# Reordered instruction streams of the gated-delta (first recurrent) layer in a four-engine pipeline

## The reference, cut to what matters

```python
q = silu(causal_dwconv(x @ Wq, qcw, qcb))       # 4 taps; k and v alike
k = k.reshape(B, T, H, DK) * DK ** (-0.5)
alpha, beta = sigmoid(x @ Wa + ba), sigmoid(x @ Wb + bb)
def step(S, inps):
    qt, kt, vt, at, bt = inps
    err = einsum('bhvk,bhk->bhv', S, kt) - vt
    S = at * S - bt * (err[..., None] * kt[:, :, None, :])
    return S, einsum('bhvk,bhk->bhv', S, qt)
o = (o - mean(o)) * rsqrt(var(o) + 1e-05) * ln_w + ln_b
return (o * sigmoid(x @ Wg)) @ Wo
```

## Time and profile before

| what | value |
|---|---|
| runs | 3175.97, 3179.49, 3179.65 us; median 3179.49 |
| the profiled execution | 3177.65 us, span 3175.9 us, mean granted PE clock 0.991 |
| busy PE / PEld / DVE / ACT / POOL | 97% / 80% / 64% / 52% / 39% |
| the layer that the change touches | PE from 402.4 us (first projection) to about 1870 us |

### The profile page before, as it was taken

One profiled execution on the slowest core, in us unless ns is written; L12 is line 12 of the kernel. 1 busy time (PEld: TensorE's weight loads), 2 busy tenths in 40 slices (PEclk: granted clock), 3 DMA queues, 4 the chain that ended last, 5 costly groups with the idle time before them and its releaser, 6 DMA issues. The chain is left out here.

```text
span 3175.9 us, 61451 instructions
## 1 busy us (share of the span) xinstructions
PE 3094.5 (97%) x23984; PEld 2550.1 (80%) x23984; DVE 2044.6 (64%) x3598; ACT 1648.3 (52%) x3880; POOL 1245.6 (39%) x2223
## 2 busy tenths in 40 slices
PE   8999989999999999999999999999999999999998
PEld 6888868888888888888788778778888888888887
DVE  5212267778777787777777743655666666666666
ACT  4221357777777777777777743343433333222222
POOL 2322335555455555555455434422333322222212
PEclk9999999999999999999999989999999999999999
DMA  2100121111111111111111145410010111000004
GB/s 89 33 21 26 60 66 37 49 45 55 51 48 45 55 50 44 51 51 45 51 48 45 54 137 162 130 44 31 27 30 27 31 43 33 24 21 27 24 17 159
DMA packets 130243, 165.70 MB, mean 52 GB/s; under 512 B 9936, under 2 KB 72144, under 8 KB 129920
## 3 DMA queue, kind: packets, MB, share of 16 engines
q1 hardware_dynamic: 120592, 144.49, 14.8%
q10 hardware_dynamic: 9296, 17.04, 1.5%
q0 software_dynamic: 64, 0.23, 0.0%
HBM read 127.91 MB, written 33.82 MB: 51 GB/s over the span
## 5 line engine op out<-in xcount | busy, mean ns | idle before, releaser
L1466 DVE SCALAR_TENSOR_TENSOR b_zt<-b_rx,b_cw,b_zt 128x512 f32<-128x512 f32 x576 | 472.2, 820 | 24.0 <-POOL b_rx L1665 4.0
L70 PE MATMUL bank<-b_XH,b_wh 128*128 128x512 f32 x1024 | 468.6, 458 | 13.1 <-ACT b_zt L1222 11.7
L72 PE MATMUL bank<-b_XH,b_wl 128*128 128x512 f32 x1024 | 405.5, 396 | 0.0
L71 PE MATMUL bank<-b_XL,b_wh 128*128 128x512 f32 x1024 | 403.0, 394 | 0.0
L70 PE MATMUL bank<-b_XH,b_qh 128*128 128x512 f32 x1024 | 399.3, 390 | 1.4 <-DVE b_g L2580 1.4
L71 PE MATMUL bank<-b_XL,b_qh 128*128 128x512 f32 x1024 | 398.9, 390 | 0.0
L72 PE MATMUL bank<-b_XH,b_ql 128*128 128x512 f32 x1024 | 398.7, 389 | 0.0
L2679 POOL TENSOR_TENSOR b_QHL<-b_qhd,b_QHH 128x512 fp32r<-128x512 f32 x128 | 181.8, 1424 | 476.4 <-ACT b_QHH L2458 474.0
L1710 POOL TENSOR_TENSOR b_PR<-b_A,b_T 128x15 f32<-128x15 f32 (+7 forms) x480 | 179.6, 374 | 188.3 <-issue 153.3
L2458 ACT CAST b_QHH<-b_qhd 128x512 fp32r<-128x512 f32 x128 | 79.5, 623 | 308.0 <-PE bank L72 186.4
L72 PEld LDWEIGHTS bank<-b_XH,b_wl 128*128 128x128 f32 x1024 | 193.2, 189 | 44.8
(11 more groups left out here) (249 smaller groups left out, 7567.3 us busy)
## 6 DMA issues: line engine op xcount, KB each, us to landing
b_abc<-tmp_a SPq DMA_DIRECT2D x64, 256.0 KB, 3.8
b_gbc<-tmp_g SPq DMA_DIRECT2D x64, 256.0 KB, 3.8
tmp_og<-b_gg SPq DMA_DIRECT2D x64, 256.0 KB, 2.1
b_mo<-tmp_og SPq DMA_DIRECT2D x64, 256.0 KB, 3.1
b_wr<-in_Wk SPq DMA_DIRECT2D x16, 256.0 KB, 4.3
b_wr<-in_Wq SPq DMA_DIRECT2D x16, 256.0 KB, 4.6
b_wr<-in_Wv SPq DMA_DIRECT2D x16, 256.0 KB, 2.6
b_wr<-in_Wg SPq DMA_DIRECT2D x16, 256.0 KB, 2.7
```

The lines of the kernel that those rows point to most:

```text
L70: e.do.matmul(out, wh, xh, start=first and k == 0, stop=False)
L71: e.do.matmul(out, wh, xl, start=False, stop=False)
L72: m = e.do.matmul(out, wl, xh, start=False, stop=last and k == n - 1)
L1466: e.do.scalar_tensor_tensor(out=z[:, :], in0=rx[:, j:j + 512], scalar=cw[:, u // 2, KIND[name[0]], j:j + 1], in1=z[:, :], op0=ALU.mult, op ...
```

## The change

Every engine's list is permuted; no instruction is added, removed or resized. The loops of PE, ACT, POOL and SP also start at another point of the round, and so does DVE's, which then needs one round less; that by itself leaves the order of the instructions as it was. What differs once that turning is taken out:
- **Projections**: same cyclic order (k0, g1, v0, q0, k1, q1, v1, g0). Banks 0 to 3 are dealt out anew.
- **PE**: `scores(2)` and `scores(3)` come ahead of and behind `inverse8_second`, before `turn(0)`; `chain2(0)` moves behind piece 3 of g0; `turn_kv(3)` moves from behind piece 3 of k0 to ahead of `chain3(0)`; `turn_kv(1)` moves up to `chain2(1)`; `turn_kv(2)` moves up to `chain1(3)`; `chain2(3)` one projection piece up; `chain3(3)` directly behind `chain4(3)`, ahead of `inverse3`.
- **DVE**: the decays spread differently; `gated(1)` ahead of `chain3(1)`; `chain3(3)` ahead of `taps(q0)`.
- **POOL**: `decayed_q(1)` of a unit moves from behind `decayed_q(0)` to a place between the first and second `root` of the following round; `root(2)` now stands ahead of `cut_next("q")` (before: behind it); `cut_next("g")` moves from ahead of `decayed_q(1)` to behind the next `rows(14)`; `cut_next("v")` and `decayed_q(0)` stay last ahead of `rows(0)`; `ones` moves behind the roots.
- **ACT**: `finish("k1")`, `finish("q1")` ahead of `out7(1)`; `cut_next` calls moved; `turned(1)` and `turned_kv(3)` ahead of `chain4(0)`; `sums(0)`, `sums(1)` together ahead of `turned_kv(0)`.
- **SP**: `products(1)` of a unit moves one round later, `decays(0)` of the next unit stands ahead of `products(0)`.

```diff
@@ -685,12 +685,12 @@
 
 
 
-PROJECTIONS = (("q1", 1), ("v1", 1), ("g0", 2), ("k0", 0), ("g1", 2), ("v0", 0), ("q0", 0), ("k1", 0))
+PROJECTIONS = (("g0", 2), ("k0", 0), ("g1", 2), ("v0", 0), ("q0", 0), ("k1", 0), ("q1", 0), ("v1", 0))
 
 TURNS = (
-    ("kv2", 2, 2), ("s3", 2, 0), ("s4a", 2, 2), ("s5", 2, 2), ("sc0", 1, 0), ("s6", 2, 2),
-    ("s7a", 2, 1), ("s78", 2, 2), ("sc1", 1, 3), ("turn0", 3, 0), ("sc2", 1, 1), ("sc3", 1, 0),
-    ("turn1", 3, 2), ("kv3", 2, 0), ("kv0", 1, 3), ("kv1", 1, 2),
+    ("sc0", 1, 3), ("s6", 2, 0), ("s7a", 2, 1), ("s78", 2, 2), ("sc1", 1, 0), ("sc2", 1, 1),
+    ("sc3", 1, 3), ("turn0", 3, 0), ("kv3", 2, 1), ("turn1", 3, 0), ("kv0", 1, 3), ("kv1", 1, 2),
+    ("kv2", 1, 3), ("s3", 1, 2), ("s4a", 1, 0), ("s5", 1, 1),
 )
 ROUNDS = NU + 3
 P_ORDER = [(i - lag, n) for i in range(ROUNDS) for n, lag in PROJECTIONS if 0 <= i - lag < NU]
@@ -891,17 +891,17 @@
     e.wait_ge("dn", 48)
     for i in range(NU + 4):
         store(i - 4, 0)
-        decays(i - 1, 0)
+        decays(i - 1, 1)
         store(i - 4, 1)
         ahead(i - 3, 1)
         ahead(i - 2, 0)
+        load_next("k", i - 1)
+        products(i - 2, 1)
+        load_next("q", i - 1)
         load_next("v", i - 1)
-        decays(i - 1, 1)
+        decays(i, 0)
         products(i - 1, 0)
         load_next("g", i - 1)
-        products(i - 1, 1)
-        load_next("k", i)
-        load_next("q", i)
 
 
 def attn0_pe(e, k, t, mt):
@@ -1117,26 +1117,6 @@
             mix0_out(e, k, mt, 0, c, js)
 
     for i in range(NU + 3):
-        project(i - 1, "q0", 2, 3)
-        chain2(i - 3, 3)
-        ahead(i - 3, 3)
-        project(i - 1, "q0", 3, 4)
-        project(i - 1, "k1", 1, 2)
-        turn_kv(i - 2, 2)
-        project(i - 1, "k1", 2, 3)
-        chain4(i - 3, 3)
-        project(i - 1, "q1", 0, 1)
-        inverse3(i - 2)
-        chain3(i - 3, 3)
-        ahead(i - 3, 4)
-        project(i - 1, "q1", 1, 2)
-        inverse4(i - 2, 0, 4)
-        project(i - 1, "k1", 3, 4)
-        project(i - 1, "q1", 2, 3)
-        inverse4(i - 2, 4, 8)
-        project(i - 1, "q1", 3, 4)
-        project(i - 1, "v1", 0, 1)
-        inverse5(i - 2)
         scores(i - 1, 0)
         inverse6(i - 2)
         project(i - 1, "v1", 1, 2)
@@ -1148,30 +1128,30 @@
         inverse78(i - 2)
         scores(i - 1, 1)
         project(i - 2, "g0", 1, 2)
+        scores(i - 1, 2)
         inverse8_second(i - 2)
+        scores(i - 1, 3)
         turn(i - 3, 0)
-        scores(i - 1, 2)
+        project(i - 2, "g0", 2, 3)
         chain2(i - 2, 0)
-        scores(i - 1, 3)
-        project(i - 2, "g0", 2, 3)
         project(i, "k0", 0, 1)
+        turn_kv(i - 2, 3)
         chain3(i - 2, 0)
         chain4(i - 2, 0)
         project(i, "k0", 1, 2)
         turn(i - 3, 1)
         project(i - 2, "g0", 3, 4)
+        project(i, "k0", 2, 3)
         chain1(i - 2, 1)
-        project(i, "k0", 2, 3)
-        turn_kv(i - 2, 3)
         project(i, "k0", 3, 4)
+        turn_kv(i - 1, 0)
         chain2(i - 2, 1)
-        turn_kv(i - 1, 0)
+        turn_kv(i - 1, 1)
         project(i - 2, "g1", 0, 1)
         chain4(i - 2, 1)
         chain3(i - 2, 1)
         project(i, "v0", 0, 1)
         project(i - 2, "g1", 1, 2)
-        turn_kv(i - 1, 1)
         chain1(i - 2, 2)
         project(i, "v0", 1, 2)
         project(i - 2, "g1", 2, 3)
@@ -1182,12 +1162,32 @@
         chain4(i - 2, 2)
         chain3(i - 2, 2)
         ahead(i - 2, 1)
+        project(i, "q0", 0, 1)
         project(i, "v0", 3, 4)
-        project(i, "q0", 0, 1)
         chain1(i - 2, 3)
         ahead(i - 2, 2)
+        turn_kv(i - 1, 2)
         project(i, "q0", 1, 2)
+        chain2(i - 2, 3)
+        ahead(i - 2, 3)
+        project(i, "q0", 2, 3)
         project(i, "k1", 0, 1)
+        project(i, "q0", 3, 4)
+        project(i, "k1", 1, 2)
+        chain4(i - 2, 3)
+        chain3(i - 2, 3)
+        ahead(i - 2, 4)
+        project(i, "k1", 2, 3)
+        project(i, "q1", 0, 1)
+        inverse3(i - 1)
+        project(i, "q1", 1, 2)
+        inverse4(i - 1, 0, 4)
+        project(i, "k1", 3, 4)
+        project(i, "q1", 2, 3)
+        inverse4(i - 1, 4, 8)
+        project(i, "q1", 3, 4)
+        project(i, "v1", 0, 1)
+        inverse5(i - 1)
 
 
 def attn0_act(e, k, t, mt):
@@ -1392,59 +1392,59 @@
     e.wait_ge("dn", 48)
     for i in range(NU + 3):
         sums(i - 3, 0)
-        chain4(i - 3, 1)
-        turned_kv(i - 2, 1)
-        finish(i - 2, "v1")
+        sums(i - 3, 1)
+        turned_kv(i - 2, 0)
         chain2(i - 3, 2)
         ahead(i - 3, 1)
+        ahead(i - 3, 2)
+        turned_kv(i - 2, 1)
         gate(i - 3, 1)
-        sums(i - 3, 1)
-        ahead(i - 3, 2)
         chain4(i - 3, 2)
-        taken(i - 1, "v0")
         sums(i - 3, 2)
         ahead(i - 3, 3)
+        taken(i - 1, "v0")
+        finish(i - 1, "k0")
         cut_next("k", i - 1)
-        finish(i - 1, "k0")
+        chain2(i - 3, 3)
+        ahead(i - 3, 4)
         spread(i - 2, 0)
         spread(i - 2, 1)
-        chain2(i - 3, 3)
-        ahead(i - 3, 4)
         taken(i - 1, "q0")
+        turned_kv(i - 2, 2)
+        chain4(i - 3, 3)
+        out3(i - 2)
         finish(i - 1, "v0")
-        turned_kv(i - 2, 2)
-        out3(i - 2)
-        chain4(i - 3, 3)
         sums(i - 3, 3)
         ahead(i - 3, 5)
         taken(i - 1, "k1")
         finish(i - 1, "q0")
+        cut_next("q", i - 1)
         taken(i - 1, "q1")
         out5(i - 2)
-        cut_next("q", i - 1)
         lower4(i - 2)
         placed6(i - 2)
         placed4(i - 2)
         out7(i - 2, 0)
-        cut_next("v", i - 1)
-        out7(i - 2, 1)
         finish(i - 1, "k1")
         finish(i - 1, "q1")
+        out7(i - 2, 1)
+        cut_next("v", i - 1)
+        taken(i - 1, "v1")
         placed8(i - 2)
         ahead(i - 2, 0)
         turned(i - 3, 0)
-        taken(i - 1, "v1")
         chain2(i - 2, 0)
-        cut_next("g", i - 1)
         diagonal(i - 1, 0)
         diagonal(i - 1, 2)
+        turned_kv(i - 2, 3)
+        turned(i - 3, 1)
         chain4(i - 2, 0)
-        turned(i - 3, 1)
         gate(i - 2, 0)
         chain2(i - 2, 1)
+        cut_next("g", i - 1)
         taken(i, "k0")
-        turned_kv(i - 2, 3)
-        turned_kv(i - 1, 0)
+        chain4(i - 2, 1)
+        finish(i - 1, "v1")
 
 
 def attn0_dve(e, k, t, mt):
@@ -1599,49 +1599,49 @@
     for d in range(3):
         i = e.do.memset(t[f"D{d}"][:, 0:1], 0.0)
     i.then_inc(S["ini"], 1)
-    for i in range(NU + 3):
-        chain1(i - 2, 0)
-        scaled(i - 3, 0)
-        masked(i - 1, 0)
-        masked(i - 1, 1)
-        decay(i - 1, 3)
-        masked(i - 1, 2)
-        masked(i - 1, 3)
-        decay(i - 1, 4)
-        decay(i - 1, 5)
-        decay(i - 1, 6)
-        masked(i - 1, 4)
-        masked(i - 1, 5)
-        decay(i - 1, 7)
-        masked(i - 1, 6)
-        masked(i - 1, 7)
-        scaled(i - 3, 1)
-        gated(i - 3, 0)
-        chain3(i - 2, 0)
-        sixteens(i - 1)
-        chain1(i - 2, 1)
-        taps(i - 1, "v1")
+    for i in range(NU + 2):
         chain3(i - 2, 1)
-        gated(i - 3, 1)
+        decay(i, 0)
         chain1(i - 2, 2)
         ahead(i - 2, 0, 1)
+        decay(i, 1)
         taps(i, "k0")
         chain3(i - 2, 2)
         ahead(i - 2, 1, 2)
         chain1(i - 2, 3)
         ahead(i - 2, 2, 4)
+        decay(i, 2)
         taps(i, "v0")
-        decay(i, 0)
         blocks(i - 1)
-        decay(i, 1)
-        decay(i, 2)
+        chain3(i - 2, 3)
+        ahead(i - 2, 4, 6)
         taps(i, "q0")
         first_guess(i - 2)
-        chain3(i - 2, 3)
-        ahead(i - 2, 4, 6)
         added4(i - 1)
         taps(i, "k1")
         taps(i, "q1")
+        chain1(i - 1, 0)
+        scaled(i - 2, 0)
+        masked(i, 0)
+        masked(i, 1)
+        decay(i, 3)
+        masked(i, 2)
+        decay(i, 4)
+        decay(i, 5)
+        masked(i, 3)
+        masked(i, 4)
+        decay(i, 6)
+        decay(i, 7)
+        masked(i, 5)
+        masked(i, 6)
+        masked(i, 7)
+        scaled(i - 2, 1)
+        gated(i - 2, 0)
+        chain3(i - 1, 0)
+        sixteens(i)
+        chain1(i - 1, 1)
+        taps(i, "v1")
+        gated(i - 2, 1)
 
 
 def attn0_pool(e, k, t, mt):
@@ -1743,39 +1743,39 @@
 
     e.wait_ge("dn", 48)
     for i in range(NU + 3):
+        rows(i - 2, 0)
+        rows(i - 2, 2)
+        tail(i - 2, "v1")
         rows(i - 2, 4)
         rows(i - 2, 6)
         halo(i - 1, "v0")
         rows(i - 2, 8)
-        tail(i - 1, "k0")
         rows(i - 2, 10)
         rows(i - 2, 12)
+        rows(i - 2, 14)
+        tail(i - 1, "k0")
+        cut_next("g", i - 2)
         halo(i - 1, "q0")
-        rows(i - 2, 14)
+        off_diagonal(i - 2)
         tail(i - 1, "v0")
-        off_diagonal(i - 2)
+        cut_next("k", i - 1)
         tail(i - 1, "q0")
         halo(i - 1, "k1")
-        cut_next("k", i - 1)
-        ones(i - 1)
-        halo(i - 1, "q1")
```

(18 more changed lines are left out.)

## The result

The changed kernel takes 3153.41 us, the median of 6 runs (3149.00 to 3156.89), beside 3178.33 for the kernel before on the same chip (6 runs, 3174.30 to 3179.65): a ratio of 0.9924, 95% interval 0.9915 to 0.9934, or 24.9 us less. Forecast were 3165 and a range of 3157 to 3176.

The account below looks back on a forecast made before the run. PE, busy 97%, was taken as the bound, losing time in weight rounds waiting at turn(1) for DVE's scaled(1). Terms -14.7 + 1 + 0 = -13.7 us on 3177.65 gave 3164.0, stated as 3165 for run spread; range 3157 to 3176.

Parts of the forecast that it names:

- the third root: POOL's late root(2) delays scaled(0) by 0.67 us, but masked waits for PE anyway: costs the kernel nothing.
- Term 1: POOL's collision with DVE's scaled(1) in 14 weight rounds: the 1.05 us wait at turn(1) goes, -14.7 us.
- term 5: Fill and tail: 0 us, bounds -2 and +2 each; PE's 4.4 us of waits without releaser may change by -3 to +3.
- Term 2: PE's own stream, new neighbours of steps: about +0.03 us a round, +1 us in all, bounds -16 and +7.
- Term 3: Serial chain, gaps from chain1 to chain2 of chunks 1 and 3 shrink to 1.6 us: 0 us, bound +19.
- Its rival: Slower through the short chain gap: sixteens still runs on DVE when chain1(1) delivers, R(1) late; 3196 us, chance 0.10.
- Term 4: Other moved calls on POOL, SP and ACT: each has slack enough, so 0 us.
- 2: The collision moves instead of going, scaled(1) late in all rounds: 3182 us, or 3174 in half the rounds; chance 0.15.
- 3: The short gap in the chain makes DVE's R(1) late: 31 us for 1 us a round, 3196 us; chance 0.10.
- Rival 4: Smaller or larger gain: PE's own stream comes out at its low half, or stalls without releaser vanish; 3158 us, chance 0.08.

Follow-up runs that it names:

- root_ahead: The kernel before with only root(2) moved ahead of cut_next("q") on POOL: 3178.83 us, ratio 1.0004 to the kernel before.
- g_away: The kernel before with only POOL's cut_next("g") moved behind the next rows(14): 3164.29 us, ratio 0.9957 to the kernel before.
- product_thrice: The changed kernel with POOL making decayed_q(0) three times, same values: 3198.34 us, ratio 1.0063 to the kernel before.
- after_again: The changed kernel, unchanged, executed once more for a second profile: 3148.36 us.
- pe_act_back: The changed kernel with PE's and ACT's lists (and PE's tables) of before; DVE, POOL and SP stay changed: 3178.68 us, ratio 1.0006 to the kernel before.
- root_behind: The changed kernel with root(2) put back behind cut_next("q") on POOL: 3150.37 us, ratio 0.9917 to the kernel before.
- pe_back: The changed kernel with PE's list and two tables of before, other engines as changed: 3220.23 us, ratio 1.0134 to the kernel before.
- scores_together: The changed kernel with scores(3) right behind scores(2), both ahead of inverse8_second, on PE alone: 3150.99 us, ratio 0.9915 to the kernel before.
- after_shift: The changed kernel with 128 already-met semaphore waits put ahead of PE's list: 3154.37 us, ratio 0.9927 to the kernel before.

## Why the prediction was right and wrong

- **What bounds the kernel, and the third root**: right. PE in weight rounds was the only steady loss; the third root costs nothing (root_ahead 1.0004).
- **Term 1**: the mechanism was right, `scaled(1)` ends beside a product in all rounds, 2.08 us long, with slack (g_away, product_thrice), and the wait is gone. The size was short, and this is the first of the two steps that failed (the other is in term 5): it took 1.05 us a weight round from the wait at `turn(1)`, and the rounds gave 1.34, so 18.8 us and not 14.7. The late `scaled(1)` made PE slow a second time, at `chain2(1)`, in a row of the weight loads' waits that the prediction had not read; that is 0.11 of the missing 0.29 us. The prediction also named the wrong neighbour: the first operation beside the slow `scaled(1)` was the low part of g, and moving that alone gave 1.19 us a round (g_away). It had the better number before it: the two windows of the earlier trace rows differ by 1.32 us, at an equal number of matmuls, and only 1.05 of that was explained. Had the sum taken the whole of it as the price of a weight round, the forecast would have been about 3161.
- **Term 2**: right. Forecast +0.03 us a round, measured +0.04 in the rounds without weights, and -0.02 in after_again, so not to be told from nothing; `scores(2)` 0.955 and `scores(3)` 0.968 against 0.96 each; `turn(0)` and `chain2(0)` fell by 0.14 and 0.08.
- **Term 3**: right at 0, but closer than it looked: R of chunk 1 has 0.3 us to spare in the rounds without weights and 0.02 to 0.14 in the weight rounds, where the walk had left 0.4. Its rival is real, too: pe_act_back shows it at 1.2 us a weight round as soon as one cast stands in the wrong place.
- **Term 4**: the sum is right and the reasoning was not. It counted each move of ACT and SP at nothing by the slack of the kernel before, as if they were independent. The four mixed kernels show that they are the other halves of the moves on PE and POOL: PE's new list among the old ones costs 55 us, PE's and ACT's new lists among the old ones 63; PE's old list among the new ones costs 67; and with PE's and ACT's old lists among the new ones all of the gain is lost.
- **Term 5**: too small, the second step that failed. The fill gave 1.4 us and is real (109.1 to 110.0 in four further executions of changed lists, 110.2 to 112.5 in five with the old ones): a product left the side of the first taps, and the granted clock came back sooner. The tail gave 0.4. The stalls without releaser gave 4.4, over the bound of 3: the row L983 alone, 4.4 us, was read for all of them, while start to start there were 10.0, and 4.3 of these in one round, which has no like in the changed kernel. Of the 10.2 us by which the profiled execution beat the sum (23.9 against 13.7), term 1 is 4.1, the stalls are 4.4, fill and tail 1.8, and all else -0.1.
- **Rivals**: 2 and 3 did not come. Rival 4 named the direction and, with 3158, was nearest. Of its two reasons, term 2 at its low end did not happen; the stalls shrank by 4.4 us, but didn't vanish, and the rest came from term 1 and the fill. The range was too narrow below since its low end took term 1 as capped by one wait. It doesn't hold what it says either: the low bound of term 2 alone, -16, would have led to 3148 and the high bound of term 3, +19, to 3184, while the range ends at 3157 and 3176. With term 1 at its measured 18.8 the sum gives 3161, inside the range; it takes the stalls and the fill to leave it.

The stalls' 4.4 us are not an effect that the change aims at: they go by which step stands at a place of PE's stream, and perhaps by what the other engines do then (pe_back, pe_act_back). Another order with the same merits could lose them again; this is luck as far as the forecast goes.

No version tried beats the changed kernel by more than its interval: root_behind and scores_together lie 3.0 and 2.4 us below, after_shift 1.0 above.

## What to carry to other kernels

When two kinds of round do the same work, the difference of their lengths is the price to explain, to the last tenth; a wait read from one row is only a part of it, and the weight loads' waits are to be read beside the matmuls'. To find what holds an operation up, begin the other engine's timeline ahead of the operation's start, not in its middle. Behind a long stall look at the granted clock as well, and then at whether a later wait takes up what it costs. In a kernel with one hand-written list for each engine, a move that "costs nothing" is often what another move needs: test the smallest part alone (here one POOL call gave half the gain), and don't expect one engine's new list to run with the others' old ones. A large elementwise product on POOL is placed by what DVE runs beside it, not by POOL's own idle time.

## What the runs showed of the hardware that was not expected

Which DVE work a POOL operation holds up depends on its kind. Timelines of DVE and POOL, changed kernel, ahead of the round at 1253.43:

```profile
1248.75 0.41 DVE L1477 TENSOR_TENSOR_SCAN b_D<-b_abc,b_cst 128x128 f32<-128x128 f32 x1
1249.08 0.46 DVE L1489 SCALAR_TENSOR_TENSOR b_XPA<-bank,b_coef,b_D 128x256 f32<-128x256 f32 x1
1249.45 1.61 DVE L1477 TENSOR_TENSOR_SCAN b_D<-b_abc,b_cst 128x128 f32<-128x128 f32 x2
...
1251.76 0.72 DVE L1477 TENSOR_TENSOR_SCAN b_D<-b_abc,b_cst 128x128 f32<-128x128 f32 x2
```

```profile
1249.19 1.27 POOL L814 TENSOR_TENSOR b_wl<-b_wr,b_wh 128x512 fp32r<-128x512 f32 x1 [1.64 <-ACT b_wh L808]
```

The `masked` operation at 1249.08, whose large input comes from a bank, runs beside the low part at its usual 0.46, and the low part keeps its 1.27; the two scans behind it, with both inputs in SBUF, take 1.61 instead of 0.72. The hold works both ways: in pe_act_back the product took 1.92 us, not 1.28, where `scaled(1)` was still running at its start and `gated(0)` followed. Both agree with what the Trainium skill (SBUF — State Buffer, SBUF: two separate sides) says of the shared port pair: that among others a DVE operation with two SBUF inputs takes it, and that whichever starts first keeps it. Not expected at all were the stalls of PE at places 1024 instructions apart, or a multiple of it, in both lists.
